# Moving the down products of two gated MLPs into the next run of a hand-ordered four-layer kernel

## The reference

```python
# layers 1 and 3, shortened
for direction in (forward, backward):
    hst = hst * exp(dt_t * A) + dt_t * B_t * x_t      # 32 states in layer 1, 64 in layer 3
    y_t = einsum('bdn,bn->bd', hst, C_t)
x = x + gate1 * (fwd + bwd)
h = norm(x) * (1 + scale) + shift
x = x + gate2 * ((silu(h @ w1) * (h @ w2)) @ w3)      # inner width 384 in layer 1, 512 in layer 3
```

## Time and profile before

| | us |
|---|---|
| median of 3 executions | 4444.14 (4440.59 to 4447.8) |
| the profiled execution | 4434.66 |
| its span from first to last instruction | 4432.9 |
| DVE busy | 4007.4 (90%) |
| PE busy | 4148.3 (94%) |
| ACT busy | 3865.3 (87%) |
| POOL busy | 3623.7 (82%) |

### The profile page before, as it was taken

How to read it: one execution, slowest core, us unless ns; L and a number is a source line. 1 busy time by engine, 2 the same in 40 slices (tenths; PEclk the granted TensorE clock), 3 DMA queues, 4 the chain that set the end, 5 groups by cost and what they waited for, 6 DMA issues and landing times.

```text
span 4432.9 us, 109964 instructions
## 1 busy us (share of the span) xinstructions
PE 4148.3 (94%) x45790; PEld 3230.5 (73%) x45790; DVE 4007.4 (90%) x3859; ACT 3865.3 (87%) x6050; POOL 3623.7 (82%) x1328
## 2 busy tenths in 40 slices
PE   9999899899899988999989999999999999999998
PEld 6457677677677764458877777778777778777777
DVE  6669999999999976659999999999999999999996
ACT  4569899899899964569999999999999999999995
POOL 3339898798889973349999998999998999988995
PEclk9999999999999999999999999999999999999999
DMA  4012122121122221032242422422422423323221
GB/s 168 1 29 68 58 66 66 53 59 67 57 60 67 65 78 41 1 44 82 86 80 83 87 67 77 83 77 82 83 76 74 81 83 94 66 81 67 76 79 40
DMA packets 241501, 305.18 MB, mean 69 GB/s; under 512 B 116449, under 2 KB 175713, under 8 KB 241009
## 3 DMA queue, kind: packets, MB, share of 16 engines
q1 hardware_dynamic: 241008, 298.15, 24.5%
HBM read 289.84 MB, written 8.26 MB: 67 GB/s over the span
## 4 chain that ended last, share of the span: by engine, by line
PE 39%; ACT 37%; DVE 15%; issue 7%; POOL 1%; DVEq 0%; DMA 0%; SPq 0%; POOLq 0%; ACTq 0%
ACT weights_c L1800 10%; PE psum L863 9%; DVE work L2316 8%; PE psum L1152 8%; PE psum L1134 7%; ACT work L1817 7%; PE psum L1131 7%; ACT work L1800 7%; PE psum L1279 5%; ACT weights_c L1817 5%; DVE weights_c L2316 4%; ACT L1498 2%; ACT modulation L1800 2%; PE psum L1362 1%; PE psum L1075 1%
## 5 line engine op out<-in xcount | busy, mean ns | idle before, releaser
L2739 POOL TENSOR_TENSOR work<-work,weights_a 128x2048 f32<-128x2048 f32 x512 | 1977.0, 3872 | 139.9 <-DVE work L2316 106.6
L2316 DVE TENSOR_TENSOR_SCAN work<-weights_c,psum 128x512 f32<-128x512 f32 x1316 | 1509.0, 1203 | 81.0 <-PE psum L1134 69.3
L2739 POOL TENSOR_TENSOR weights_c<-weights_c,weights_a 128x2048 f32<-128x2048 f32 x256 | 989.4, 3873 | 50.2 <-DVE weights_c L2316 49.6
L1134 PE MATMUL psum<-ident,work 128*128 128x128 f32 x5464 | 932.6, 273 | 0.0
L1800 ACT ACTIVATE work<-work,decay 128x504 f32<-128x504 f32 x1172 | 817.8, 709 | 53.4 <-DVE weights_c L2316 27.4
L1134 PE MATMUL psum<-ident,weights_c 128*128 128x128 f32 x3752 | 694.5, 275 | 0.0
L2316 DVE TENSOR_TENSOR_SCAN work<-work,psum 128x512 f32<-128x512 f32 x586 | 675.2, 1201 | 20.1 <-PE psum L1134 16.9
L2316 DVE TENSOR_TENSOR_SCAN weights_c<-work,psum 128x512 f32<-128x512 f32 x586 | 675.7, 1201 | 19.1 <-PE psum L1134 18.5
L1152 PE MATMUL psum<-ident,work 64*128 64x64 f32 x16800 | 659.0, 229 | 10.6 <-POOL work L2739 7.6
L1134 PEld LDWEIGHTS psum<-ident,work 128*128 128x128 f32 x5464 | 668.2, 142 | 0.0
L1152 PEld LDWEIGHTS psum<-ident,work 64*128 64x128 f32 x16800 | 586.7, 140 | 99.8 <-issue 75.4
(11 more groups left out here) (221 smaller groups left out, 6453.9 us busy)
## 6 DMA issues: line engine op xcount, KB each, us to landing
weights_a<-c_rows SPq DMA_DIRECT2D x384, 512.0 KB, 3.7
work<-b_diagonals SPq DMA_DIRECT2D x240, 128.0 KB, 2.2
weights_c<-b_diagonals SPq DMA_DIRECT2D x112, 128.0 KB, 2.1
b_diagonals<-weights_c SPq DMA_DIRECT2D x1, 4096.0 KB, 18.1
weights_c<-in_L_cond_fwd_in_w SPq DMA_DIRECT2D x8, 512.0 KB, 5.2
weights_c<-in_L_cond_fwd_xproj_w SPq DMA_DIRECT2D x4, 1024.0 KB, 7.3
weights_c<-in_L_cond_bwd_in_w SPq DMA_DIRECT2D x8, 512.0 KB, 5.4
weights_c<-in_L_cond_bwd_xproj_w SPq DMA_DIRECT2D x4, 1024.0 KB, 7.5
```

Source lines behind the costliest of these rows:

```text
L1134: last = nc.tensor.transpose(PS[:, bank, t * P:(t + 1) * P], buf["scaled"][s % INPUTS][t][:, j * P:(j + 1) * P], IDENT[:, :])
L2316: v.tensor_tensor_scan(buf["ring"][s % RING][:, along, j], buf["decay"][q % DECAYS[l]][:, along], PS[:, 4 + q % LOOKAHEAD, along], 0.0, AL ...
L2739: g.tensor_tensor(state, state, row.unsqueeze(2).broadcast_to([P, T, DC]), ALU.mult).then_inc(ss["prod_ready"], 1)
```

## The change

In layer 3 `down0` leaves the end of runs 2, 4, 6 and stands ahead of `down1` at the start of runs 3, 5, 7. In layer 1 both down products of blocks 0 and 1 leave the ends of runs 3 and 5 and stand at the start of runs 4 and 6, whose plan now starts at step 2 rather than 12. `down0` and `down1` of runs 7 and 8 of layer 1 stay. The up results of layer 1 go to three tiles that are free then (the decay rates of layer 3, a spent part of the modulation tensor, and the first half of H1B) rather than to a buffer which the next run's inputs overwrite. The core of the diff:

```diff
+def downs1(r):
+
+    return r // 2 - 2 if r in (4, 6) else r // 2 - 1 if r in (RUNS - 1, RUNS) else None
+
+
 def copier(r, name):
...
     if r >= 3 and r % 2:
-        jobs += [("down1", DC, 3)]
+        jobs += [(f"down{c}", DC, 3) for c in range(KC)]
     if r >= 1:
...
         jobs += [(f"dt{j}", DC, 3) for j in range(DC)] + [("bc", DC, 3 if closes(r) else 9)]
-    if closes(r):
-        jobs += [("down0", DC, 5)]
     if head:
...
     jobs = [(f"down{c}", MLP // P, 3) for c in range(KC)] if r == 0 else []
+    if tail and head and downs1(r) is not None:
+        jobs += [("down0", HIDDEN1, 3), ("down1", HIDDEN1, 3)]
     if tail:
...
         jobs += [(f"dt{j}", 1, 4) for j in range(DC)]
-    if gated:
+    if gated and downs1(r) is not None:
         jobs += [("down0", HIDDEN1, 3), ("down1", HIDDEN1, 8)]
...
-PIPES = {1: Pipe(32, 2, pipe_jobs1, 1, lambda r: 2 if r % 2 else 12 if r >= 2 else -IN_GAP),
+PIPES = {1: Pipe(32, 2, pipe_jobs1, 1, lambda r: 2 if r % 2 or r in (4, 6) else 12 if r >= 2 else -IN_GAP),
...
-            v += ["yt"] + [f"ytb{j}" for j in range(DC)] + ["out0", "x0", "out1", "x1"]
+            v += ["yt"] + (["down0", "end0", "down1", "end1"] if head and downs1(r) is not None else []) + [f"ytb{j}" for j in range(DC)] + ["out0", "x0", "out1", "x1"]
...
-        GLU1 = lambda r: region(WORK, 9216, HIDDEN1, T) if r < RUNS else region(WC, 13824, HIDDEN1, T)
+        GLU1 = lambda r: [A3.rearrange("p d j n -> p (d j n)"), region(SPENT, 0, T), H1B[:, 0, :]] if r < RUNS else [
+            region(WC, 13824 + T * k, T) for k in range(HIDDEN1)]
...
+                    def down(made_in):
+                        for c in range(KC):
+                            yield from product(f"down{c}", [by("dve", f"end{c}")], chunk(WM1["w3"], c),
+                                               GLU1(made_in), lambda k: made("dve", f"up{k}@{made_in}"))
+
                     if r == 0:
                         yield from held_down(r, product, by)
+                    if ends and head and downs1(r) is not None:
+                        yield from down(r - 1)
                     if ends:
...
-                    if gated:
-                        for c in range(KC):
-                            yield from product(f"down{c}", [by("dve", f"end{c}")], chunk(WM1["w3"], c),
-                                               [GLU1(r)[:, k, :] for k in range(HIDDEN1)],
-                                               lambda k: made("dve", f"up{k}@{r}"))
+                    if gated and downs1(r) is not None:
+                        yield from down(r)
...
-                        yield from down(1, r - 1)
+                        for c in range(KC):
+                            yield from down(c, r - 1)
...
-                    if closes(r):
-                        yield from down(0, r)
...
                                                    in1=x[:, c, :], op0=ALU.add, op1=ALU.add).then_inc(done(f"end{c}"), 1)
+                    def close(b):
+                        for c in range(KC):
+                            yield from gated(r, plan, bank, done, f"down{c}", f"end{c}", c, b, 3)
+
                     if ends:
-                        yield from tail(r, plan, bank, done, YT1(r), Z1, f"silu_z@{r - 2}", nb)
+                        yield from tail(r, plan, bank, done, YT1(r), Z1, f"silu_z@{r - 2}", nb,
+                                        close(downs1(r)) if head and downs1(r) is not None else ())
                     if norms:
...
-                            v.tensor_tensor(GLU1(r)[:, j, :], SG1(r)[:, j, :], bank[f"up{j}"],
+                            v.tensor_tensor(GLU1(r)[j], SG1(r)[:, j, :], bank[f"up{j}"],
                                             ALU.mult).then_inc(done(f"up{j}"), 1)
                     if head and r < 0:
                         yield from rectify(r, plan, bank, done, "L1_cond_dt_proj_b")
-                    if mlp:
-                        for c in range(KC):
-                            yield from gated(r, plan, bank, done, f"down{c}", f"end{c}", c, r // 2 - 1, 3)
+                    if mlp and downs1(r) is not None:
+                        yield from close(downs1(r))
...
-                                        close(1, r // 2 - 1) if r >= 3 and r % 2 else ())
+                                        close(r // 2 - 1) if r >= 3 and r % 2 else ())
...
-                        yield from norm(r, plan, done, 3, H1B, nb, f"up2@{r - 1}" if r >= 4 else None)
+                        yield from norm(r, plan, done, 3, H1B, nb, f"down1@{r if head else r - 1}" if r >= 4 else None)
                     if r % 2 and head and r >= 0:
                         for j in range(DC):
                             for shift, scaled in ((2, "near"), (3, "far")):
```

13 lines of the change are left out of this document (5 added, 8 removed).

## The result

The changed kernel takes 4451.67 us (median of 20 executions, 4448.98 to 4460.88) against 4443.97 us before (20 executions, 4436.18 to 4450.37): ratio 1.0024, 95% interval 1.0018 to 1.0030, slower by 0.24% (the medians lie 7.7 us apart, the means 11.0). The forecast was 4439.7, a gain of 4.4 us, with a range of 4427 to 4451. The profiled execution took 4451.33 us.

The account below looks back on a forecast made before the run. A run's time was taken as DVE's work plus DVE's idle time. The terms -15.3 + 9.9 - 7.0 + 8.0 gave -4.4 us: 4430.3 on the profiled execution, 4439.7 in terms of the median, range 4427 to 4451.

Parts of the forecast that it names:

- Layer 1, runs 3 and 5: Two pairs of DVE operations gone (-2.35 us), stalls gone (-1.44), lost catching up +0.3: -3.5 each, -7.0 together.
- ACT and POOL lose 4 us in which they caught up behind `softplus`; I put +0.3: Layer 1 runs 3 and 5: less time for ACT and POOL to catch up behind `softplus`, priced at +0.3 us a run.
- The two stalls of 1.04 and 0.40: Layer 1 runs 3 and 5: DVE's waits at the down products' bursts of three matmuls disappear, -1.44 us a run.
- Layer 1, runs 4 and 6: Two pairs of DVE operations added (+2.35 us), burst +1.0, `down1` +0.7: +4.0 each, +8.0 for both (6 to 13).
- +0.7 (0.3 to 3): Heads of layer 1's runs 4 and 6: DVE time lost as PE stands some 4 us at `down1` for bank 7.
- the burst's +1.0: Heads of layer 1's runs 4 and 6: `down0`'s three matmuls in one burst behind an adding of sums, +1.0 us.
- The clock rival: Granted clock falls at heads of layer 1's runs 4 and 6, 2.3 us more each: +0.2, 4444.3 us; 15 in 100.
- Layer 3, runs 2, 4, 6: Each loses a DVE pair (-1.17 us) and gains looser matmul spacing (-2.6); shorter waits -4.0 in all: -15.3 together.
- The wait moved to `bt`: End of layer 3's even runs: `bt` waits instead of `down0`, well under 1.5 us; 1.5 us of DVE idle taken.
- Layer 3, runs 3, 5, 7: Each gets a DVE pair (+1.17 us), with head and plan costs: 4.1 in runs 3 and 5, 1.7 in 7: +9.9.
- The closed-up plan: Layer 3 runs 3 and 5: denser matmuls, 0.349 a step instead of 0.330, cost +1.9 us over 150 steps.
- The rival of a bank-7 chain in the odd heads: Layer 3 odd runs: bank-7 handovers waiting for DVE cost 4.5 us a run more: +9, 4453 us; 8 in 100.

Follow-up runs that it names:

- kernel with lighter ACT work: Changed kernel with Exp for Softplus and without its two table loads in layer 1's runs 3 and 5: 4445.13 us, ratio 1.0004.
- the one with the old steps: Changed kernel with the removed jobs' gap kept in layer 1's runs 3 and 5, other jobs at their steps of before: 4449.98 us, ratio 1.0021.
- the last kernel: Changed kernel with `down0` ahead of `yt`, `silu_z` mid-run in layer 3's runs 0, 3, 5, and gap 2 for 3 behind `down1`: 4437.66 us.

## Why the prediction was wrong

**What bounds the kernel.** Right: DVE's own work was the same to 1.0 us, and the whole outcome is its idle time. The sum had the wrong sign because layer 1's two terms were too good by 11.5 us together.

**Layer 1, runs 3 and 5 (predicted -7.0, measured -2.9).** The failed step is "ACT and POOL lose 4 us in which they caught up behind `softplus`; I put +0.3". The mechanism had been seen and given a tenth of its price. In the changed kernel PE stands 3.22 us for ACT and DVE 4.4 us where it was idle 1.3 before, so 3.1 us more, and 3.5 in run 5. About half of it is the longer wait (the stand grew by 1.5 and 1.8 us), the other half, 1.6 us, the low clock behind it. The kernel with lighter ACT work (a stand shorter by 1.2 and 1.5 us) and the one with the old steps (nearly the same stand) show that the wait is for ACT's work. The two stalls of 1.04 and 0.40 did go, as predicted, but 0.7 us of new idle time stands at scan 90.

**Layer 1, runs 4 and 6 (predicted +8.0, measured +15.4).** The moved work, +2.35 a run, was right. The stand of PE at `down1` was foreseen at "some 4 us" (measured 3.02), but the step that turned it into DVE time, "+0.7 (0.3 to 3)", failed: with the burst's +1.0 it was to be 1.7 and measured 3.1 more than before in run 4 and 4.0 in run 6. The clock rival, with 15 in 100, had the granted clock right (0.57 behind the stand). That the difference in run 6, 2.3 us, is also its price is luck: the 2.3 had been read from two waits that were not of one length (below). Putting `down0`'s operations ahead of `yt` took away stand and low clock together and gave 3.5 us a run, so the two aren't priced apart at this place. The burst alone was rightly sized (0.94 for 1.0). Not in the sum at all were 1.9 us a run of idle time in steps 32 to 40: the steps were listed ahead of the prediction as "the rest where it was within two steps", and one step was enough. One gap smaller by 1 took it away.

**Layer 3, runs 2, 4, 6 (predicted -15.3, measured -12.6).** Steps 160 to 192 of run 4 take 37.90 us, 1.184 a step (predicted 1.18). The wait moved to `bt` and shrank, as said. What was missed is again ACT: `silu_z`'s block behind it, 1.4 us of DVE idle time at scan 247 in runs 2 and 4 and 0.7 in run 6, and in run 4 the middle block, 2.5 us more idle time in steps 128 to 144. So the sum is nearer than its parts: run 4 was to gain 6.6 us and gained 0.8, while run 2 was to gain 4.4 and gained 7.3, of which 2.0 are a gap at its second scan in the profile before; the kernel with the layer-1 part alone, the same in layer 3, does not have that gap.

**Layer 3, runs 3, 5, 7 (predicted +9.9, measured +9.7).** The size was right and its split partly wrong. The head cost 0.9 to 1.0 us as put. The closed-up plan was to cost 1.9 us over the run; steps 32 to 224 cost 0.3 us or less, and 1.0 and 1.8 us in runs 3 and 5 lie at the end, where DVE waits 2.27 us for ACT behind `silu_z` in run 5; moving `silu_z` gave 2.0 to 2.2 us of it back in each of runs 3 and 5. The rival of a bank-7 chain in the odd heads did not happen.

**The clock rule of the Trainium skill** ("TensorE: Matmul & The Clock Gate", Part 1, What's actually happening: low is the default to which an idle array returns). By it the heads pay each time. The trace agrees here: the clock was low behind the stand of both heads in all five kernels that have it, the runs' mean is 0.99, and 1.00 with the stand removed. Elsewhere it does not hold each time: behind the 3.21 us of the last kernel the clock stayed high.

The prediction set against the clock rival that PE "had stood 2.8 us before in both" waits of the earlier trace rows, and that this length did nothing in run 6. That reading is wrong. In run 6 of the kernel before PE stands 2.18 us at `down0`:

```profile
4035.81 1.12 PE L863 MATMUL psum<-scratch,weights_c 128*128 128x512 f32 x2 [2.18 <-ACT weights_c L1744]
```

So the argument against the rival falls. Of the 2.3 us that it took as the price of the low clock, 0.62 are the longer stand of run 4 (2.80 less 2.18); the 1.6 that are left are what the stands at `dtx2` give too.

**The chances.** Slower had 10 in 100, and the one rival on that side had DVE and bank 7 in it. No case had ACT, which at 87% was taken to have room wherever it is needed; at the ends of layer 1's odd runs it had some 2 us, and in layer 3 `bt` waits for it.
